# Moving the rank's one-hot and the norm's application from VectorE to GpSimd, a shorter verdict, and an opening with two DMA queues

## The reference, cut to what matters

```python
x = x + attn_a(_layernorm(x), ...)
# in attn_a, for each of 32 batches and 16 heads of width 8:
topk = max(1, int(Tx * 0.3))                    # 76 of 256
scores = einsum('bhid,bhjd->bhij', q, k) * scale
topk_scores, indices = jax.lax.top_k(scores, topk)
masked = full_like(scores, -inf).at[..., indices].set(topk_scores)
attn = softmax(masked)
out = einsum('bhij,bhjd->bhid', attn, v)
return out @ W_out.T + b_out
```

## Time and profile before

| | |
|---|---|
| median of three runs | 5192.93 us |
| profiled execution, device time | 5187.39 us |
| its span, first to last instruction | 5185.5 us |
| opening block | 0 to 35.6 us |
| attention a | 35.6 to about 2440 us |
| busy over the span: PE, DVE, ACT, POOL | 87%, 77%, 61%, 49% |

### The profile page before, as it was taken

How to read it: one execution, slowest core, us unless ns; L and a number is a source line. 1 busy time by engine, 2 the same in 40 slices (tenths; PEclk the granted TensorE clock), 3 DMA queues, 4 the chain that set the end, 5 groups by cost and what they waited for, 6 DMA issues and landing times. The chain is left out here.

```text
span 5185.5 us, 120998 instructions
## 1 busy us (share of the span) xinstructions
PE 4522.9 (87%) x34302; PEld 3170.4 (61%) x34302; DVE 4012.6 (77%) x14195; ACT 3174.4 (61%) x10274; POOL 2564.9 (49%) x3089
## 2 busy tenths in 40 slices
PE   4688888788878878887999999899999998999998
PEld 3344444444434444443788888666666666888887
DVE  4899999999989999997788888555555555888886
ACT  4688888888868888885222222477676774222222
POOL 1567667676657676676444444211111112444444
PEclk8566667666656676666999999999999999999999
DMA  3000000000000000000444444100000001444444
GB/s 76 10 11 13 13 10 13 10 13 14 10 10 14 10 13 10 14 14 4 83 82 84 86 87 87 25 11 11 11 11 11 11 11 40 87 87 86 82 82 98
DMA packets 359400, 188.83 MB, mean 36 GB/s; under 512 B 190736, under 2 KB 347824, under 8 KB 358960
## 3 DMA queue, kind: packets, MB, share of 16 engines
q1 hardware_dynamic: 358960, 183.74, 17.5%
HBM read 147.24 MB, written 11.01 MB: 31 GB/s over the span
## 5 line engine op out<-in xcount | busy, mean ns | idle before, releaser
L874 ACT ACTIVATE junk<-SS,nt 128x256 bf16<-128x256 f32 x3072 | 1517.0, 501 | 157.1 <-POOL nt L478 107.4
L495 POOL TENSOR_SCALAR gone<-SS,mid 128x256 bf16<-128x256 f32 x1024 | 1178.6, 1167 | 561.2 <-DVEq L1067 453.2
L1241 POOL TENSOR_TENSOR f_hid<-f_g_m,f_cbs 128x256 f32<-128x256 f32 x1024 | 743.7, 726 | 849.9 <-DVE f_g_m L1486 666.4
L1341 ACT ACTIVATE f_th<-bank 128x256 f32<-128x256 f32 x1088 | 416.9, 383 | 1146.0 <-PE bank L1272 1146.0
L1271 PE MATMUL bank<-f_xTf,wgT 128*128 128x256 f32 x2176 | 693.2, 400 | 51.4 <-DVE f_g_m L1486 36.0
L1887 DVE TENSOR_REDUCE nmxb<-bank 128x2 f32<-128x512 f32 x512 | 329.4, 685 | 475.9 <-PE bank L1659 475.9
L1272 PE MATMUL bank<-f_xTf,wuT 128*128 128x256 f32 x2176 | 652.3, 382 | 0.0
L1303 PEld LDWEIGHTS bank<-wdT,f_hid 128*128 128x128 f32 x4096 | 602.4, 192 | 65.0 <-POOL f_hid L1241 11.6
L1303 PE MATMUL bank<-wdT,f_hid 128*128 128x128 f32 x4096 | 630.4, 277 | 9.5 <-POOL f_hid L1241 9.3
L652 PE MATMUL bank<-k,q 32*128 32x256 f32 x2048 | 422.9, 548 | 218.9 <-DVE SS L988 216.7
L874 ACT ACTIVATION_READ_ACCUMULATOR junk<-SS,nt 128x1 f32 x3072 | 596.6, 194 | 0.0
(11 more groups left out here) (229 smaller groups left out, 7644.8 us busy)
## 6 DMA issues: line engine op xcount, KB each, us to landing
f_cbs<-f_shares SPq DMA_DIRECT2D x512, 256.0 KB, 5.8
q4x<-q SPq DMA_DIRECT2D x64, 256.0 KB, 2.3
k4x<-k SPq DMA_DIRECT2D x64, 128.0 KB, 2.1
qrow<-q_rows SPq DMA_DIRECT2D x512, 8.0 KB
q_rows<-qTb SPq DMA_DIRECT2D x32, 128.0 KB, 1.7
out_dram<-xres SPq DMA_DIRECT2D x4, 1024.0 KB, 9.4
q4x<-max_rows SPq DMA_DIRECT2D x128, 4.0 KB
f_shares<-f_combT SPq DMA_DIRECT2D x64, 32.0 KB, 1.5
```

Source lines behind the costliest of these rows:

```text
L495: last = pool.tensor_scalar(gone[:, h % 4, i, :], SS[:, (u - lag) % 4, c, :], mid[:, (u - lag) % 4, 0, c:c + 1], 0.0, ALU.subtract, ALU.min)
L874: nc.scalar.activation(junk[:, c % 2, :], SS[:, uu % 4, c, :], ACT.Sign, bias=bias(c), accum_out=acc[:, k, uu % 4, c:c + 1]).then_inc(s["s ...
L1241: pool.tensor_tensor(hid[:, e % NBUF, :], g_m[:, e % NBUF, :], cbs[:, par, e, :], ALU.mult).then_inc(s["hid"], 1)
```

## The change

1. The one-hot leaves VectorE. GpSimd builds it after kk and after "upper", as two operations (rank differences, then equality to zero), into a buffer with two places; a new semaphore "hot" tells VectorE.
2. The verdict has three operations in place of five: level (first value against the threshold), apart (`max(mid1, 1e-6) >= mid0`), and the union of both with its accumulation. The logic is the same, only negated. The reduction into mid signals by a semaphore of its own, "picked", for which GpSimd waits in place of "failed".
3. The norm is applied by GpSimd: two operations over 128x256 behind rstd in `front`, in place of two of VectorE over 128x128 each. `front` stands in front of `outsiders(3, (6, 7))` and of u1. It also waits for TensorE's earlier use of xn.
4. The residual addition (L1106) is one operation over both halves, not two.
5. In the opening, nine of the small loads are issued by ScalarE's queue; b_out and the gate's bias, the expert weights and the rest of x move from the opening block to SP's queue of the next block, ahead of the 16 px loads (L545). TensorE waits for 24 loads, not 26.

```diff
-                for i, w in enumerate((W_qkv[0:P, :], W_qkv[P:2 * P, :], W_qkv[2 * P:3 * P, :], W_out,
-                                       Wq, Wk, Wv, Wp, sh_gate, sh_up, sh_down)):
+                for i, w in enumerate((W_qkv[0:P, :], W_qkv[P:2 * P, :], W_qkv[2 * P:3 * P, :], W_out)):
                     sp.dma_start(nat[:, i, :], w).then_inc(s_w, 16)
-                sp.dma_start(gnat[:, :], gate_w).then_inc(s_w, 16)
-                sp.dma_start(pnat[:, :, :], ...).then_inc(s_w, 16)
...
             def _(act):
+                for i, w in enumerate((Wq, Wk, Wv, Wp, sh_gate, sh_up, sh_down)):
+                    nc.scalar.dma_start(nat[:, 4 + i, :], w).then_inc(s_w, 16)
+                nc.scalar.dma_start(gnat[:, :], gate_w).then_inc(s_w, 16)
+                nc.scalar.dma_start(pnat[:, :, :], ...).then_inc(s_w, 16)
...
                 def front(b):
                     pool.wait_ge(s["mv"], b + 1)
                     own.link(pool.tensor_tensor(vareps[:, :], mv[:, :, 1], eps_t[:, :], ALU.add))
-                    pool.tensor_tensor(rstd[:, :], vareps[:, :], half_pow[:, :], ALU.pow).then_inc(s["rstd"], 1)
+                    own.link(pool.tensor_tensor(rstd[:, :], vareps[:, :], half_pow[:, :], ALU.pow))
+                    wait(pool, s["m0c"], 0 if isinstance(b, int) and b == 0 else m0_before(b - 1, "xT"))
+                    pool.sem_inc(s["pgate"], 1)
+                    own.link(pool.tensor_tensor(xn[:, :, :], xpair(b), mv[:, :, 0:1].to_broadcast([P, HALVES, D]), ALU.subtract))
+                    pool.tensor_tensor(xn[:, :, :], xn[:, :, :], rstd[:, :].unsqueeze(2).to_broadcast([P, HALVES, D]), ALU.mult).then_inc(s["xn"], 1)
...
                         wait(pool, s["signs"], signs(t - 1, "c3"))
-                        wait(pool, s["failed"], t - 2)
+                        wait(pool, s["picked"], t - 2)
...
                         pool.sem_inc(s["upper"], 1)
+                        own.link(pool.tensor_tensor(oh[:, u % 2, :, :], iota[:, :, :], kk[:, u % 2, :].unsqueeze(2).to_broadcast([P, GT, 15]),
+                                                    ALU.subtract))
+                        pool.tensor_scalar(oh[:, u % 2, :, :], oh[:, u % 2, :, :], 0.0, None, ALU.is_equal).then_inc(s["hot"], 1)
                     if even and ahead:
                         front(bb + 1)
                     outsiders(3, (6, 7))
...
             def _(sp):
+                sp.dma_start(bo[:, :], ...).then_inc(s_b, 16)
+                sp.dma_start(gbias[:, :], ...).then_inc(s_b, 16)
+                sp.dma_start(stage[:, 0], ...).then_inc(s_stage, 16)
+                sp.dma_start(stage[:, 1], ...).then_inc(s_stage, 16)
+                sp.dma_start(stage[:, 2]..., ...).then_inc(s_stage, 16)
+                n = (BATCH - 2) * HALVES // 3
+                for c in range(3):
+                    k = slice(2 * HALVES + c * n, 2 * HALVES + (c + 1) * n)
+                    sp.dma_start(xres[:, k, :], x_dram[:, k, :]).then_inc(s_xr, 16)
+                sp.wait_ge(s_b, 32)
                 sp.wait_ge(s_pext, 1)
...
-                        hot = own.mark(V.tensor_tensor(oh[:, :, :], iota[:, :, :], kk[:, y, :]..., ALU.is_equal))
-                        yield
-                        own.need(own.n)
+                        wait(dve, s["hot"], t - 1)
+                        if own.n:
+                            own.need(own.n)
...
-                        apart = own.mark(V.tensor_tensor(nxt[:, :], mid[:, z2, 1, :], mid[:, z2, 0, :], ALU.is_lt))
-                        yield
-                        own.need(apart)
-                        positive = own.mark(V.scalar_tensor_tensor(tmp[:, :], mid[:, z2, 0, :], 1.0e-6, nxt[:, :], ALU.is_gt, ALU.mult))
-                        yield
-                        own.need(positive)
-                        both = own.mark(V.tensor_tensor(fine[:, z2, :], fine[:, z2, :], tmp[:, :], ALU.mult))
-                        yield
-                        own.need(both)
-                        V.tensor_scalar(fail[:, 0:GT], fine[:, z2, :], 0.0, 0.0, ALU.is_equal, ALU.add, accum_out=fail[:, GT:GT + 1]).then_inc(s["failed"], 1)
+                        wait(dve, s["picked"], t - 1)
+                        dve.sem_inc(s["gate"], 1)
+                        apart = own.mark(V.scalar_tensor_tensor(nxt[:, :], mid[:, z2, 1, :], 1.0e-6, mid[:, z2, 0, :], ALU.max, ALU.is_ge))
+                        yield
+                        own.need(apart)
+                        V.scalar_tensor_tensor(fail[:, 0:GT], nxt[:, :], 0.0, tmp[:, :], ALU.add, ALU.max, accum_out=fail[:, GT:GT + 1]).then_inc(s["failed"], 1)
...
-                        if h == 1 and even and front:
-                            normed(bb + 1)
```

53 lines of the change are left out of this document (22 added, 31 removed).

## The result

The changed kernel takes 5344.5 us (median, 5339.9 to 5350.5) against 5195.6 us for the kernel before in the same comparison (5181.8 to 5204.1): a ratio of 1.029, 95% interval 1.0265 to 1.0315. It is 2.9% slower. The forecast was no change that can be told.

What follows compares the result with a forecast made beforehand. VectorE (92% busy) looked like attention a's bound, with GpSimd on the path from c1 to c2 in even steps; one queue's issue time ended the opening. 5187.4 - 17 (opening) + 10 (attention a) = 5180 us, range 5122 to 5233.

Steps and rivals of the forecast that it cites:

- the next three steps: Attention a's loop: the third step's lateness of 2.4 us falls to 0.65 per four steps, +10 over 15.5 fours.
- Opening: Before attention a: next block starts 17.9 us earlier (bounds 16 and 19.5), norm on GpSimd costs 0.9; sum -17.
- Rival 4: Opening doesn't shorten: loads land no sooner, or moved loads hold up step 0 or 2; 5197 us, chance 0.05.
- VectorE's saving: Attention a's loop: one-hot, two small operations, norm and merged residual save VectorE 3.5 us per four steps.
- GpSimd's additions: Attention a's loop: one-hot adds GpSimd 1.95 us a step, norm 1.6 in even steps, 3.55 there before u1.
- Rival 3: GpSimd's equality is cheap, 0.33 us; four steps come out at -0.6; 5161 us, chance 0.10.
- The third step: Attention a's loop, u = 2: nt and c2 3.55 us later, VectorE +2.35, rest of step about 2.4 late.
- The first: VectorE is the bound in attention a: c2's delay is hidden, the whole 54 us come home; 5116 us, chance 0.24.
- The second: GpSimd's queue takes over in both even steps of attention a: 4.7 us more per four; 5243 us, chance 0.19.

Runs made afterwards that it cites:

- e9: Kernel before with the change's opening and merged residual addition, verdict still in five operations, code placed as before: 5170.1 us, ratio 0.9958.
- e7: Changed kernel with one-hot and norm back on VectorE, plus 19 never-executed instructions so the experts 1 code stands as before: 5127.6 us, ratio 0.9878.
- e4: Changed kernel with the norm back on VectorE, the one-hot staying on GpSimd, code placed as before: 5147.9 us, ratio 0.9913.
- e10: e7 without its 19 padding instructions, so the experts 1 loop begins at 2008: 5291.8 us in one run.
- e1_padded: Changed kernel with 31 never-executed VectorE instructions, so the experts 1 loop stands at 2027 as before: 5207.7 us, ratio 1.0031.
- e11: e7 with the one-hot on GpSimd behind u1, ahead of the wait for okay: 5160.7 us, ratio 0.9951.

## Why the prediction was wrong, step by step

Two steps failed. The larger is a term that the sum doesn't have: it takes every stage outside the opening and attention a to keep its time, and gives no reason; experts 1 became 136 us longer by the place of its code. The other is "the next three steps", which let four steps cost 0.65 us more; they cost 3.0.

*Opening: right, a little low.* Forecast -17, measured -20.3, just outside its bounds of 16 to 19.5. bv left the queue at 6.89 (forecast 7.0), but TensorE started 3.0 us later, not 5.2 to 5.6; the prediction named this case ("some 2 us less") and didn't take it. SP was free 36.9 us into the block (forecast 37). Rival 4 is out. (Its own terms, 12.2 to 12.6, 5.1 and 0.7, give 18.0 to 18.4 for the start of the block, not 17.8; the measured 15.4 is earlier than either.)

*VectorE's saving: right in its total, by luck in its parts.* Odd steps became 0.54 us shorter (forecast 0.6), and VectorE's share of the stretch fell from 92% to 90% (forecast 89). But of the forecast 0.6 the one-hot was to bring 0.43 and the verdict 0.16. By the table the verdict alone takes the odd steps from 38.0 to 37.4 (e9, e7), and moving the one-hot takes off 0.2 more at most (e4 37.2) and nothing in the changed kernel (37.5).

*GpSimd's additions: the mechanism right, the sizes high.* Groups of GpSimd in the changed kernel, which answer to the earlier trace rows:

```profile
L511 POOL TENSOR_SCALAR oh<-oh 128x240 f32<-128x240 f32 x64 | 54.4, 851 | 5.6
...
L509 POOL TENSOR_TENSOR oh<-iota,kk 128x240 f32<-128x240 f32 x64 | 38.4, 600 | 11.7 <-POOL kk L507 11.7
...
L434 POOL TENSOR_TENSOR xn<-xn,rstd 128x256 f32<-128x256 f32 x32 | 20.4, 637 | 2.5
L433 POOL TENSOR_TENSOR xn<-xres,mv 128x256 f32<-128x256 f32 x32 | 20.3, 636 | 11.4 <-POOL rstd L430 11.4
```

The equality takes 0.85 us (taken at 1.1, bounds 0.33 and 1.17), the subtraction 0.60 (0.68), each half of the norm 0.64 (0.73). The Trainium skill, GPSIMD Engine Reference, section 4.1 Engine selection, puts two inputs at about twice VectorE's time and one input roughly at line rate. The trace does not agree here either: the one-input operation is the slower one, 0.85 against 0.60 over the same 240 columns. In the third step nt is 2.8 us late at the median, not 3.55. Rival 3 would have needed 0.33.

*The third step: its first half right.* Okay is 1.5 us later (forecast 2.35), and VectorE waits 1.3 us in front of its MAX8 at h == 4 (forecast about 2), as the chain nt, c2, flags, okay wanted.

*"Recovered over the next three steps": this is what failed.* The prediction let the lateness of 2.4 us shrink to 0.65 per four steps. By the table of steps four of them cost +3.0 (+1.0, -0.5, +3.1, -0.5). (The step-by-step subtraction should also have ended at 0.5 and not 0.65.) The sentence that ScalarE's copy of q moves and "TensorE waits for it" was true, and was priced as a delay. It is a gap as well, and behind it TensorE runs at half its clock while the exponentials wait for its products. By the numbers above the clock is about half of what the third steps lost, the delay the other half. The number 0.67 stood in the earlier trace rows and was read as a constant. Worse, the step that was followed, t = 30, was one of the six slow third steps of the kernel before: it is at clock 0.50 throughout in the rows above. Eight others were at the high clock and had some 3 us to lose, and one step's timeline couldn't show that.

*The verdict: right in direction, far too small.* It was priced as two operations of 0.08 us a step, 10 us in all. e7 against e9 says 52 us in the profiled executions, of which 30 x 0.55 = 17 are shorter odd steps; the first steps account for 26 (14 of 15 at the high clock instead of 4) and the third for 7, which makes 50. By the medians it is 42, and of the 26 a part is luck of the execution, since e10 has 9 high first steps with the same instructions. Why the odd steps gain more than the operations' own time isn't shown. The two parts that the prediction argued about most, one-hot and norm, then gave all of this back and more: 74 us (80 by the medians).

*Code position: absent.* No part of the prediction asks where the loops stand once 31 instructions have gone in front of them. This is +136 of the +153 us. Without it (e1_padded) the kernel is at 5207.7, 28 us above the forecast, and the difference from before is 0.3%.

*Rivals.* The first (VectorE is the bound) falls by its own sign: VectorE does wait in front of its MAX8 at h == 4, 1.27 us in t = 30, and the 54 us didn't come home in e1_padded. ScalarE's waiting for nt was 136.6 us, against 101.8 in the same view of the kernel before. The second ended on the right side by another way: its sign was that GpSimd no longer waits for c1, and GpSimd still does.

## What to carry to other kernels

Cut a profile by stage before explaining it, and where a stage that wasn't edited has changed, look for idle time by "issue" and for packets in the instruction queues; pad or trim the code ahead of a long loop before judging an edit by its time. Work moved from a full engine to an emptier one is worth its place in the chain of waits and not its duration: here both moves to GpSimd lost, and a verdict of three operations instead of five, with its earlier signal, brought some 42 us, four times its own operations' time. Run the same executed code more than once before reading a difference of one stage of one profile: here it moved by up to 17.5 us. Read TensorE's granted clock step by step: where TensorE is near the bound and its clock changes within a step, a gap of two microseconds in front of it can cost more than its length, and one followed step must be shown to be a typical one.

## What the runs showed of the hardware

- VectorE's loop over experts, 260 instructions long, costs 9.1 to 9.8 us more per turn at some places of the program (1996, 2252, 2008) than at others (2027, 2236). The same code, moved by 31 places, differs by 136 us of 5200.
- A gap of 1.95 us in TensorE's work went with a fall of its granted clock from 1.00 to 0.54 for the stretch behind it. Gaps of 1.91 to 3.41 us at this place did so in 12 of 12 cases, gaps of 0.93 to 1.15 in none of 8, but two of 1.88 in another kernel (e11) didn't either. Filling the gap with unneeded products kept the clock at 1.00 in 12 of 14 cases. Twelve unneeded products in one step of four, put where there was little gap, came with 62 us more in all, 14 of them their own price and much of the rest in steps at a lower clock.
- The same executed instructions had 4, 10 and 11 of 15 first steps at the high clock in three kernels, 9 and 14 in two others, and attention a differed by up to 12 and 17.5 us with it. Where a kernel has four or more of either kind, its even steps at the low clock last 1.8 to 4.0 us longer than those at the high one.
- GpSimd's tensor_tensor with an input broadcast along the row took 600 to 637 ns, over 240 and 256 columns; one of two full inputs over 256 columns took 726 ns (L1241 of the kernel before), and so did one whose second input is read twice, 128 columns each time.
- Nine loads issued on ScalarE's queue and eight moved behind the first block shorten an opening by 20.3 us; what SP issues later is hidden beside the work, down to 14.16 us of issue for px.
